# Two value products in a row instead of one at a time, a ring of ten exponential buffers, and a compact layout of the stationary values

## The chip, the cores and the metric

The kernel runs on one core of one Trainium2 chip. The metric is the device time of one execution in microseconds; of several executions the median is given.

## The reference

A layer with attention and a mixture of experts runs on X of 32 batches x 256 tokens x 128 features (float32), both branches from the same normalised input:

```python
xn = _layernorm(x)
x = x + attention(xn) + experts(xn)

# attention, H = 16 heads of DK = 8
ctx = X @ We.T                                          # 16 features
influence = einsum('bqe,bke->bqk', ctx, ctx)
scores = einsum('bhqd,bhkd->bhqk', Q, K) * DK**-0.5 + 0.1 * influence[:, None]
out = softmax(scores) @ V  ->  (b, s, d) @ Wo.T

# experts: 8 of 128 -> 512 -> 128 with gelu, the best 2 of softmax(xn @ gate_w.T) for each token
```

## The kernel before

The engines' programs are written out by hand; each engine runs its own list in order, and semaphores (`wait_ge`, `then_inc`) tie the lists together. After a start (normalising, routing) the attention of batches 0 to 15 runs, then the experts (about 300 to 493 us of the profile), then the attention of batches 16 to 31, while the rows of the experts are gathered.

The attention loop runs over steps `k`, one batch a step, and in each over eight sub-steps `u` = 0 to 7. Work of several batches overlaps in a step: `b` is the batch whose scores are made, `b1_` the next one, `bo` the one before, `b3_` the third ahead. What an engine does in a step, in its order:

- TensorE (PE). At even `u`, two **plain products** for batch `b1_` (`plain(u)`, `plain(u+1)`, L1137, four matmuls each), from which only the maxima of the scores are taken. They go into the two buffers `MX[0]` and `MX[1]`; `plain(v)` waits until VectorE has reduced the product two before it (L1133). At each `u`, two **score products** for batch `b` (`shifted(0)` and `shifted(1)`, L1125, two matmuls each, score products 2u and 2u+1 of the batch) into two banks; score product n waits for the exponential n-2 (L1122). Between the two score products stand small products: those of the values at `u` = 3 (L1147, which wait for `lo_qk` of L966, since they share the bank `MISC`), the transposes of the sums `O` at `u` = 5 (L1154), those of the normalised output at `u` = 7 (L1159). After the score products: at `u` = 0 the output projection of the batch before that (L1185), at `u` = 1 the projection of queries and keys for `b3_` (L1023).
- The **value products** (`values`, L1103) multiply the exponentials by the values: four groups a batch, each of four exponentials, 8 matmuls in float32 with 32 stationary columns, which the profile shows as 16 records in four quads. Group 0 stands at the end of `u` = 2, group 1 at `u` = 4, group 2 at `u` = 6, and group 3 at `u` = 0 of the next step, behind the output projection. Groups 0 and 1 add up in the bank `PV`, are copied to `O` and are followed by groups 2 and 3 there.
- VectorE (DVE). One reduce per plain product (L948, called here the first to eighth reduce of a step), four small transposes of the maxima after the fourth and the eighth (L954), at `u` = 0 the addition of the finished output (L962) after the first reduce, at `u` = 2 `lo_qk` (L966) after the third, at `u` = 5 the reciprocal and the normalising (L972, L976) after the sixth. The reciprocal waits for the transposes of L1154.
- ScalarE (ACT). Sixteen exponentials a step (L700) into a ring `A` of eight buffers, with a wait for a value product (L696); copies of `PV` (L689) at `u` = 1 and 5, `hi_qk` (L706) at `u` = 1, the values into `V` (L716) at `u` = 3, `oT` (L731) at `u` = 7. In the first half it also converts pieces of the experts' weights.
- SyncE issues the loads and stores, GpSimd scatters rows (first half) and gathers them (second half); both are paced by counts of finished score products (`s_ex`).

In the last step, `k` = 31, there are no plain products, and the scores use six banks.

Of the kernel before, what the change touches and what calls it, by code (L numbers as in the profile page):

```python
# [19 lines left out]
F32 = mybir.dt.float32  # L20
F16 = mybir.dt.float16
# [3 lines left out]
ACT = mybir.ActivationFunctionType  # L25
AX = mybir.AxisListType

P = 128
D = 128
B = 32  # L30
S = 256
H = 16
DK = D // H
DE = D // 8
# [6 lines left out]
ET = 2 * B * S // SLOT + NE - 1  # L41
EW = -(-ET // 4)
EP = 4 * EW
NA = 8
VB = 272
DIGIT = 3
QROW, CROW, REST = (0, 9 * DK), (3 * DK, 12 * DK), 5 * DK
MROWS = ((0, 8 * DK), (8 * DK, 14 * DK))
# [2 lines left out]
WS = 2.0 ** 8  # L51
FS = 2.0 ** 10
SCALE = DK ** -0.5
CTX = (0.1 / SCALE) ** 0.5
RW = 2 * D + 2
ZROWS = 9
# [68 lines left out]
def build(nc, X, Wsmall, Wo, W12, B1, B2, out):  # L125
    with ExitStack() as ctx:
        def sb(name, shape, dt):
            return ctx.enter_context(nc.sbuf_tensor(name, shape, dt))
# [12 lines left out]
        x = sb("x", [P, NT, D], F32)  # L141
# [7 lines left out]
        b1 = sb("b1", [P, NE * FC], F32)  # L149
        stack = sb("stack", [P, 2, H, 2, S], F16)  # L150
        A = sb("A", [P, NA, 2, S], F32)
        V = sb("V", [P, 2, 4 * VB], F32)
        O = sb("O", [P, 2, 2, S], F32)
        hi_qk = sb("hi_qk", [P, 2, S], F16)
        lo_qk = sb("lo_qk", [P, 2, S], F16)
# [26 lines left out]


        stats = A[:, 0, :, :].rearrange("p h s -> p (h s)")[:, 0:NT * 6].rearrange("p (t s) -> p t s", s=6)
        zeros = A[:, 1:NA // 2, :, :].rearrange("p n h s -> p (n h s)")[:, 0:ZROWS * RW // 2]
        part_c = [A[:, NA // 2 + r, :, :].rearrange("p h s -> p (h s)").bitcast(F16).rearrange("p (a t) -> p a t", a=2) for r in range(4)]
        early = w12[:, :, :].rearrange("p a n -> p (a n)")
        taken = [0]

# [38 lines left out]
        EX, PV, MISC = bank[4:6], bank[6], bank[7]  # L228
        ring = EX + bank[0:4]

        def scores(k, n):

            return ring[n % len(ring)] if k == B - 1 else EX[n % 2]

        def head_values(par, c, g, i):

            at_ = VB * (2 * c + g % 2) - 16 * (g % 2) + 32 * (4 * (g // 2) + i)
            return V[:, par, at_:at_ + 32]


        s_x = [sem(f"s_x{q}") for q in range(4)]
# [10 lines left out]
        s_qk, s_hq, s_lq, s_cx, s_ch, s_cl, s_v, s_vc = (sem(n) for n in ("s_qk", "s_hq", "s_lq", "s_cx", "s_ch", "s_cl", "s_v", "s_vc"))  # L252
# [4 lines left out]
        s_ex, s_xp, s_pv, s_pe = (sem(n) for n in ("s_ex", "s_xp", "s_pv", "s_pe"))  # L257
# [188 lines left out]
        def _(pool):  # L446
# [36 lines left out]
            pool.memset(V[:, :, :], 0.0).then_inc(s_post, 1)  # L483
            pool.wait_ge(s_post, 4)
            for par in range(2):
                ins = pool.memset(V[:, par, :].rearrange("p (n j) -> p n j", n=4)[:, :, 0:256].rearrange("p n (j d) -> p n j d", d=32)[:, :, :, DK:DK + 1], 1.0)
            ins.then_inc(s_post, 1)

            chain = [0]
# [121 lines left out]
        def _(act):  # L611
# [59 lines left out]
            def attend(s, f, k, first_half=True):  # L671
                b, par, half = s.at(0)
                b1_, par1, _ = s.at(1)
                b3_, par3, _ = s.at(3)
                bo, paro, _ = s.at(-1)
                ch, c_lo = high_chunk(s, k, first_half), low_chunk(s, k, first_half)
                for u in range(8):
                    g = u // 2
                    if first_half and k == HALF and u in (0, 2):
                        experts.load((u // 2 + 1) * (EW // 2))  # L680
                    if first_half and k == HALF and u == 3:
                        act.wait_ge(s_small, 32)
                        act.activation(probe[:, :], ones16[0:1, 0:1], ACT.Gelu_apprx_tanh)
                    if (u == 1 and f["o"]) or (u == (6 if k == B - 1 else 5) and f["x"]):
                        bb, pp, gg = (bo, paro, 1) if u == 1 else (b, par, 0)
                        act.wait_ge(s_pv, 4 * bb + 2 * gg + 2)
                        if k is None or bb >= 2:
                            act.wait_ge(s_ot, bb - 1)
                        act.activation(O[:, pp, gg, :], PV[:, 0:S], ACT.Copy).then_inc(s_pe, 1)  # L689
                    if f["x"]:  # L690
                        for n in (2 * u, 2 * u + 1):
                            act.wait_ge(s_ex, 16 * b + n + 1)
                            if k == 0 and n == 0:
                                act.wait_ge(s_zero, 64)
                            if k != 0 or g >= 2:
                                act.wait_ge(s_pv, 4 * b + g - 1)  # L696
                            if k == 0 and n == NA // 2:
                                for sm in s_cw:
                                    act.wait_ge(sm, 96)
                            act.activation(A[:, n % NA, :, :].rearrange("p h s -> p (h s)"), scores(k, n)[:, :], ACT.Exp, scale=SCALE).then_inc(s_xp, 1)  # L700

                    if u == 1 and f["p"]:
                        act.wait_ge(s_qk, b3_ + 1)
                        if k is None or b3_ >= 1:
                            act.wait_ge(s_wr[1 - par3], 64 * (s.at(2)[2] + 1))
                        act.activation(hi_qk[:, :, :].rearrange("p a t -> p (a t)"), MISC[:, :], ACT.Copy, scale=1 / WS).then_inc(s_hq, 1)  # L706
                    if k == -1 and u == 5:
                        act.wait_ge(s_sub, 3)
                        act.activation(Ex, Dl, ACT.Exp, scale=1 / WS).then_inc(s_exp8, 1)
                        act.wait_ge(s_sub, 4)  # L710
                        act.activation(second, second, ACT.Exp, scale=1 / WS).then_inc(s_exp8, 1)
                    if u == 3 and f["m"]:
                        act.wait_ge(s_v, b1_ + 1)
                        if k is None or b1_ >= 2:
                            act.wait_ge(s_pv, 4 * b1_ - 4)
                        act.activation(V[:, par1, :].rearrange("p (n j) -> p n j", n=4)[:, :, 0:256].rearrange("p n (j d) -> p n j d", d=32)[:, :, :, 0:DK],  # L716
                                       MISC[:, 0:S].rearrange("p (n j d) -> p n j d", n=4, d=DK), ACT.Copy, scale=1 / WS).then_inc(s_vc, 1)
                    if u == 2 and c_lo is not None:
                        act.activation(w_stage[:, :], w_stage[:, :], ACT.Copy, scale=FS).then_inc(s_wsc, 1)
                    if k == 1 and u == 6:  # L720
                        act.wait_ge(s_routed, 2)
                        act.wait_ge(s_place, 2)
                    if u == 6 and ch is not None:
                        act.wait_ge(s_wst, 16 * (ch + 1))
                        dst = w12[:, 0, ch * WCH:(ch + 1) * WCH] if isinstance(ch, int) else w12[:, 0, bass.ds(ch * WCH, WCH)]
                        act.activation(dst, w_stage[:, :], ACT.Copy, scale=FS).then_inc(s_whi, 1)
                    if u == 7 and f["o"]:
                        act.wait_ge(s_oT, bo + 1)
                        if k is None or bo >= 1:
                            act.wait_ge(s_wo, bo)  # L730
                        act.activation(oT[:, :], MISC[:, 0:2 * P], ACT.Copy).then_inc(s_oTe, 1)  # L731
# [279 lines left out]
        def _(pe):  # L1011
# [75 lines left out]
            def attend(s, f, k):  # L1087
# [5 lines left out]
                def values(bb, pp, g):  # L1093

                    gg, e = g // 2, g % 2
                    pe.wait_ge(s_xp, 16 * bb + 4 * g + 4)
                    if g == 0:
                        pe.wait_ge(s_vc, bb + 1)
                    if e == 0 and (not isinstance(bb, int) or 2 * bb + gg >= 1):
                        pe.wait_ge(s_pe, 2 * bb + gg)  # L1100
                    for c in range(2):
                        for i in range(4):
                            mm = pe.matmul(PV[32 * i:32 * i + 32, 0:S], head_values(pp, c, g, i), A[:, (4 * g + 2 * c + i // 2) % NA, i % 2, :],  # L1103
                                           start=(e == 0 and c == 0), stop=(e == 1 and c == 1))
                    mm.then_inc(s_pv, 1)

# [3 lines left out]
                for u in range(8):  # L1110
# [67 lines left out]
                        pe.wait_ge(s_routed, 1)  # L1178
                        experts.load(EW)
                    if u == 0 and f["o"] and closing:  # L1180
                        values(bo, paro, 3)
                    if u == 0 and f["c"]:
                        drained(0, s, f, k)
                        for q in range(2):
                            mm = pe.matmul(MISC[:, S + q * P:S + (q + 1) * P], oT[:, q * P:(q + 1) * P], wo[:, :], start=True, stop=True)  # L1185
                        mm.then_inc(s_wo, 1)
                    if u == 0 and f["o"] and not closing:
                        values(bo, paro, 3)
                    if u == 1 and opening:
                        pe.wait_ge(s_fy, ET)  # L1190
                    if u == 1 and f["p"]:
# [3 lines left out]
                        if k == 1:  # L1195
                            pe.wait_ge(s_routed, 2)
                        project(b3_)
                    if u in ((3, 5, 7) if k == B - 1 else (2, 4, 6)) and f["x"]:
                        values(b, par, g - 1)
                    if k == 0 and u == 6:  # L1200
                        pe.wait_ge(s_vc, 2)
                        pe.wait_ge(s_te, 1)
                        pe.matmul(MISC[0:1, 0:EW], tile_of[0:EP, 0:1], digits[:, :], start=True, stop=True).then_inc(s_tile, 1)
# [78 lines left out]
```

## Time and profile before

| | us |
|---|---|
| runs shown, median of 3 | 711.17 (710.17 to 714.66) |
| the profiled execution, its own time | 710.7 |
| its span, first to last instruction | 708.9 |
| PE busy | 645.0 (91%) |
| DVE busy | 613.8 (87%) |
| ACT busy | 540.8 (76%) |
| GpSimd busy | 469.0 (66%) |
| granted TensorE clock, mean share of full speed | 0.982 |

The busy time of PE is modelled: matmuls are pipelined, and each record holds the time until its last result. Two matmuls that start 0.11 us apart each last 0.27 us, so a busy PE can still have unused places.

### The profile page before, as it was taken

The page shows a single profiled execution, that of the slowest core. Times are in us where ns is not written, and L with a number is a line of the kernel's source. Part 1 is how long each engine was busy: PE and PEld are TensorE (multiplying, and loading weights), DVE is VectorE, ACT ScalarE, POOL GpSimd, SP SyncE. Part 2 cuts the span into 40 slices and gives each one's busy share as a digit, 9 for nine tenths or more (in the row PEclk, how much of TensorE's full clock was granted, in tenths as well). Part 3 has the DMA queues.
Part 4 walks back from the last instruction along what each step waited for, and adds up shares of the span by engine and source line. Part 5 has one row for each costly group of instructions (what it writes and reads, how often), then busy time and mean ns, then how long its engine had stood idle before and what let it go on. Part 6 is the DMA issues. An engine that isn't in the chain of part 4 may idle for free.

```text
span 708.9 us, 22900 instructions
## 1 busy us (share of the span) xinstructions
PE 645.0 (91%) x7800; PEld 431.6 (61%) x7800; DVE 613.8 (87%) x1106; ACT 540.8 (76%) x1123; POOL 469.0 (66%) x542
## 2 busy tenths in 40 slices
PE   0367899999999999879999999999999999999996
PEld 0254445555555555569999999999455555555553
DVE  8979899999899899758888888887999999999991
ACT  2583478888888888758888888888787887778785
POOL 8680478687677657125566566566688888878883
PEclk9996799999999999999999999999999999999999
DMA  9859566676686776564444454543576877788742
GB/s 249 305 161 338 150 160 180 179 204 167 178 199 178 184 183 172 148 109 100 101 106 102 101 96 110 103 99 79 142 169 174 191 186 187 175 189 195 179 112 76
DMA packets 162975, 113.71 MB, mean 160 GB/s; under 512 B 72624, under 2 KB 150448, under 8 KB 162864
## 3 DMA queue, kind: packets, MB, share of 16 engines
q1 hardware_dynamic: 153632, 90.63, 51.5%
q0 software_dynamic: 8192, 16.86, 9.8%
q10 hardware_dynamic: 1040, 4.76, 1.8%
q8 instruction: 67, 1.10, 0.7%
q14 instruction: 44, 0.36, 0.2%
HBM read 55.42 MB, written 47.19 MB: 145 GB/s over the span
## 4 chain that ended last, share of the span: by engine, by line
PE 62%; DVE 16%; SPq 9%; DMA 7%; issue 4%; ACT 1%; DVEq 0%; ACTq 0%
PE bank L1243 14%; PE mx L1232 13%; PE bank L1125 12%; PE bank L1103 10%; DVE mx L948 8%; PE mx L1137 6%; DMA stack<-qk_dram 4%; PE bank L1023 2%; PE bank L1185 2%; DVE A L783 2%; SPq L322 2%; DVE lo_qk L966 2%; DMA stack<-mT 2%; SPq L326 1%; PE bank L1154 1%
## 5 line engine op out<-in xcount | busy, mean ns | idle before, releaser
L700 ACT ACTIVATE A<-bank 128x512 f32<-128x512 f32 x502 | 278.0, 597 | 57.6 <-PE bank L1125 48.7
L948 DVE TENSOR_REDUCE mx<-mx 128x4 f16<-128x1024 f32 x256 | 302.5, 1205 | 18.4 <-PE mx L1137 15.9
L571 POOL TENSOR_SCALAR rows<-rows,slot_p 128x128 f32<-128x128 f32 x142 | 112.2, 800 | 99.0 <-DVE rows L999 99.0
L1125 PE MATMUL bank<-stack 113*128 113x256 f16 x1004 | 170.1, 276 | 1.8 <-ACT A L700 0.8
L557 POOL DMA_INDIRECT slots_x<-rows,pos x128 | 124.0, 969 | 50.9 <-PE bank L1125 30.0
L601 POOL DMA_INDIRECT rows<-slots_y,pos x128 | 122.0, 953 | 37.1 <-issue 18.2
L1103 PE MATMUL bank<-A,V 128*32 128x256 f32 x2048 | 137.1, 385 | 1.8 <-ACT A L700 1.7
L744 ACT ACTIVATE rows<-mx,b 128x256 f32<-128x256 f32 x284 | 111.5, 475 | 30.2 <-PE mx L1232 29.9
L1125 PEld LDWEIGHTS bank<-stack 113*128 113x128 f16 x1004 | 73.2, 97 | 89.6 <-ACT A L700 48.7
L993 DVE TENSOR_TENSOR rows<-rows 128x512 f16<-128x512 f32 x142 | 101.2, 714 | 24.5 <-ACT rows L748 22.1
L1243 PE MATMUL bank<-w,rows 128*128 x1704 | 108.4, 220 | 4.4 <-DVE rows L993 4.4
L1243 PEld LDWEIGHTS bank<-w,rows 128*128 128x128 f16 x1704 | 102.2, 98 | 6.7 <-issue 4.9
L1232 PE MATMUL mx<-rows,w 128*128 128x256 f16 x852 | 105.1, 273 | 0.0
L1137 PE MATMUL mx<-stack 64*128 64x256 f16 (+1 forms) x1024 | 88.4, 277 | 11.8 <-DVE mx L948 5.9
L1232 PEld LDWEIGHTS mx<-rows,w 128*128 x852 | 80.6, 98 | 8.5 <-issue 0.2
L1103 PEld LDWEIGHTS bank<-A,V 128*32 128x32 f32 x2048 | 53.5, 109 | 48.5 <-issue 20.0
L1137 PEld LDWEIGHTS mx<-stack 64*128 64x128 f16 (+1 forms) x1024 | 33.4, 95 | 59.1 <-DVE mx L948 26.2
L954 DVE STREAM_TRANSPOSE mT<-mx 32x32 f16<-32x32 f16 x256 | 51.2, 200 | 4.8
L748 ACT ACTIVATE rows<-rows 128x512 f16<-128x512 f32 x71 | 44.8, 631 | 6.7
L1044 PE MATMUL mx<-ident,rows 128*128 128x128 f16 x128 | 13.9, 274 | 35.5 <-DVE rows L820 33.9
L689 ACT ACTIVATE O<-bank 128x256 f32<-128x256 f32 x64 | 24.7, 386 | 27.8 <-PE bank L1103 27.8
L989 DVE CAST rows<-rows 128x512 f16<-128x512 f32 x71 | 30.4, 428 | 12.7 <-ACT rows L744 5.7
(142 smaller groups left out, 591.4 us busy)
## 6 DMA issues: line engine op xcount, KB each, us to landing
stack<-ctx_rest SPq DMA_DIRECT2D x64, 256.0 KB
stack<-qk_dram SPq DMA_DIRECT2D x128, 96.0 KB
slots_y<-rows SPq DMA_DIRECT2D x71, 128.0 KB, 2.1
qk_dram<-hi_qk SPq DMA_DIRECT2D x64, 128.0 KB
stack<-ctx_high SPq DMA_DIRECT2D x128, 64.0 KB
slots_x<-A ACTq DMA_DIRECT2D x1, 4644.0 KB, 19.8
w_stage<-in_w SPq DMA_DIRECT2D x8, 512.0 KB
qk_dram<-lo_qk SPq DMA_DIRECT2D x64, 64.0 KB
```

The lines of the kernel that those rows point to most:

```text
L557: pool.indirect_dma_start(slots_x, bass.IndirectOffsetOnAxis(pos[j][:, t:t + 1], 0), rows[:, t, :].bitcast(F32), None).then_inc(s_scat, 16)
L571: ins = pool.tensor_scalar(ye[n % 4][:, h, :], ye[n % 4][:, h, :], slot_p[:, n // 4 % 3, n % 4, h:h + 1], None, ALU.mult)
L601: pool.indirect_dma_start(ye2[n % 2][:, m, :], None, slots_y, bass.IndirectOffsetOnAxis(pos[j][:, t:t + 1], 0)).then_inc(s_yg[n % 2][m], 16)
L700: act.activation(A[:, n % NA, :, :].rearrange("p h s -> p (h s)"), scores(k, n)[:, :], ACT.Exp, scale=SCALE).then_inc(s_xp, 1)
L744: act.activation(h32[r % 2][:, fc, :], bank[fc][:, 0:SLOT], ACT.Gelu_apprx_tanh, bias=b1[:, bass.ds(e + fc, 1)], scale=1 / FS).then_inc(s_ ...
L948: dve.tensor_reduce(mx[:, a, 8 * qt:8 * qt + 8].rearrange("q (i e w) -> q i e w", i=2, e=2)[:, :, g % 2], MX[u % 2][:, :].rearrange("q (i ...
L993: dve.tensor_tensor(lo, h, hi, ALU.subtract).then_inc(s_fl, 1)
L1103: mm = pe.matmul(PV[32 * i:32 * i + 32, 0:S], head_values(pp, c, g, i), A[:, (4 * g + 2 * c + i // 2) % NA, i % 2, :], start=(e == 0 and c ...
L1125: mm = pe.matmul(scores(k, n)[:, i * S:(i + 1) * S], stack[0:SHIFT + 1, par, h, 1, c * P:(c + 1) * P], stack[0:SHIFT + 1, par, h, 0, :], s ...
L1137: mm = pe.matmul(MX[v % 2][:, (2 * i + p) * S:(2 * i + p + 1) * S], stack[r0:r1, par1, h, 0, v % 2 * P:(v % 2 + 1) * P], stack[r0:r1, par1 ...
L1232: mm = pe.matmul(bank[fc][:, 0:SLOT], w1[:, pa, bass.ds(e + fc * P, P)], xt[r][:, pb, :], start=(n == 0), stop=(n == 2))
L1243: mm = pe.matmul(bank[6 + par][:, h * D:(h + 1) * D], hp[par][:, pa, fc, h * P:(h + 1) * P], w2[:, pb, bass.ds(e_before + fc * P, P)], sta ...
```

## The change

On PE, groups 0 and 1 of the value products now stand one behind the other at the end of `u` = 4, groups 2 and 3 one behind the other at `u` = 0 of the next step, again behind the output projection; at `u` = 2 and `u` = 6 there are none. The last step keeps its order, and so do all waits of `values` itself. The ring `A` has ten buffers and goes on from batch to batch, so that an exponential waits for the value product of ten exponentials before. `V` shrinks from 1088 to 768 columns: each 48-column place holds the values of two heads, 16 zeros apart. ACT copies the values at `u` = 4, behind the exponentials 8 and 9, instead of `u` = 3. The order of the rows of Wv is changed on the host.

```diff
-NA = 8
-VB = 272
+NA = 10
+VP = 3 * 2 * DE // 2
...
-        V = sb("V", [P, 2, 4 * VB], F32)
+        V = sb("V", [P, 2, H * VP], F32)
...
-            at_ = VB * (2 * c + g % 2) - 16 * (g % 2) + 32 * (4 * (g // 2) + i)
+            at_ = VP * (8 * c + 4 * (g // 2) + i) + 16 * (g % 2)
             return V[:, par, at_:at_ + 32]
...
-                            if k != 0 or g >= 2:
-                                act.wait_ge(s_pv, 4 * b + g - 1)
-                            if k == 0 and n == NA // 2:
+                            if 16 * b + n >= NA:
+                                act.wait_ge(s_pv, (16 * b + n - NA) // 4 + 1)
+                            if k == 0 and n == 4:
...
-                            act.activation(A[:, n % NA, :, :].rearrange("p h s -> p (h s)"), scores(k, n)[:, :], ACT.Exp, scale=SCALE).then_inc(s_xp, 1)
+                            act.activation(A[:, (16 * b + n) % NA, :, :].rearrange("p h s -> p (h s)"), scores(k, n)[:, :], ACT.Exp, scale=SCALE).then_inc(s_xp, 1)
...
-                    if u == 3 and f["m"]:
+                    if u == 4 and f["m"]:
                         act.wait_ge(s_v, b1_ + 1)
...
-                        act.activation(V[:, par1, :].rearrange("p (n j) -> p n j", n=4)[:, :, 0:256].rearrange("p n (j d) -> p n j d", d=32)[:, :, :, 0:DK],
-                                       MISC[:, 0:S].rearrange("p (n j d) -> p n j d", n=4, d=DK), ACT.Copy, scale=1 / WS).then_inc(s_vc, 1)
+                        act.activation(head_columns(par1), MISC[:, 0:S].rearrange("p (n e d) -> p n e d", e=2, d=DK), ACT.Copy, scale=1 / WS).then_inc(s_vc, 1)
...
                     if u == 0 and f["o"] and closing:
-                        values(bo, paro, 3)
+                        for n in ((3,) if bo == B - 1 else (2, 3)):
+                            values(bo, paro, n)
...
                     if u == 0 and f["o"] and not closing:
-                        values(bo, paro, 3)
+                        for n in (2, 3):
+                            values(bo, paro, n)
...
-                    if u in ((3, 5, 7) if k == B - 1 else (2, 4, 6)) and f["x"]:
+                    if f["x"] and k == B - 1 and u in (3, 5, 7):
                         values(b, par, g - 1)
+                    if f["x"] and k != B - 1 and u == 4:
+                        for n in range(2):
+                            values(b, par, n)
```

## Rows read from the trace of the kernel before

**Rows 1.** The page: busy time of the engines, and granted clock in 40 slices.
```profile
PE 645.0 (91%) x7800; PEld 431.6 (61%) x7800; DVE 613.8 (87%) x1106; ACT 540.8 (76%) x1123; POOL 469.0 (66%) x542
...
PEclk9996799999999999999999999999999999999999
```

**Rows 2.** Busy us by stretch: length, PE, PEld, DVE, ACT, POOL, clock, DMA share, GB/s.
```profile
202.13:215.25 13.12, 13.00 (x150) 6.91 (x148) 12.41 (x22) 11.04 (x22) 9.91 (x12) 1.00 0.84 208
560.00:640.00 80.00, 78.98 (x910) 43.53 (x908) 75.33 (x124) 63.73 (x129) 65.84 (x65) 1.00 0.78 184
```

**Rows 3.** Line L948: what its idle time before waited for, who waited (us, times).
```profile
  PE mx L1137: 15.9, 25
...
  PEld mx L1137: 26.2, 72
```

**Rows 4.** Timeline of DVE, one step: start, us, instruction, count, idle before.
```profile
205.39 1.23 DVE L948 TENSOR_REDUCE mx<-mx 128x4 f16<-128x1024 f32 x1 [0.50 <-PE mx L1137]
206.53 0.68 DVE L966 SCALAR_TENSOR_TENSOR lo_qk<-bank,hi_qk 128x512 f16<-128x512 f32 x1
207.13 1.22 DVE L948 TENSOR_REDUCE mx<-mx 128x4 f16<-128x1024 f32 x1
...
209.15 2.30 DVE L948 TENSOR_REDUCE mx<-mx 128x4 f16<-128x1024 f32 x2
211.38 0.34 DVE L972 RECIPROCAL rden<-bank 128x32 f32<-128x32 f32 x1
...
212.09 2.35 DVE L948 TENSOR_REDUCE mx<-mx 128x4 f16<-128x1024 f32 x2
...
218.88 1.23 DVE L948 TENSOR_REDUCE mx<-mx 128x4 f16<-128x1024 f32 x1 [0.87 <-PE mx L1137]
```

**Rows 5.** Timeline of DVE, end of the next step and its successor's third reduce.
```profile
225.58 2.35 DVE L948 TENSOR_REDUCE mx<-mx 128x4 f16<-128x1024 f32 x2
...
231.99 1.23 DVE L948 TENSOR_REDUCE mx<-mx 128x4 f16<-128x1024 f32 x1 [0.49 <-issue]
```

**Rows 6.** Timeline of PE over the same boundary: value product, scores, projection, plain products.
```profile
229.35 1.07 PE L1103 MATMUL bank<-A,V 128*32 128x256 f32 x16
230.36 0.61 PE L1125 MATMUL bank<-stack 113*128 113x256 f16 x4
230.81 0.82 PE L1023 MATMUL bank<-xT,ws 128*128 128x256 f16 x6
231.56 0.61 PE L1137 MATMUL mx<-stack 64*128 64x256 f16 x8
```

**Rows 7.** Timeline of PE, the fourth and fifth sub-steps (u = 4, 5).
```profile
208.40 0.39 PE L1137 MATMUL mx<-stack 64*128 64x256 f16 x4
208.72 0.61 PE L1125 MATMUL bank<-stack 113*128 113x256 f16 x4
209.26 1.07 PE L1103 MATMUL bank<-A,V 128*32 128x256 f32 x16
210.27 0.39 PE L1125 MATMUL bank<-stack 113*128 113x256 f16 x2
210.50 0.60 PE L1154 MATMUL bank<-ident,O 128*128 128x128 f32 x4
```

**Rows 8.** Timeline of the weight loads (PEld): the second plain product at u = 4.
```profile
208.39 0.12 PEld L1137 LDWEIGHTS mx<-stack 64*128 64x128 f16 x4 [0.36 <-DVE mx L948]
```

**Rows 9.** Timeline of PE in two very short windows: third and fourth quad.
```profile
206.49 0.40 PE L1103 MATMUL bank<-A,V 128*32 128x256 f32 x4
...
206.71 0.40 PE L1103 MATMUL bank<-A,V 128*32 128x256 f32 x4
```

**Rows 10.** Timeline of PE, u = 3: the products of the values.
```profile
207.27 0.51 PE L1147 MATMUL bank<-ws,xT 128*128 128x128 f16 x6
```

**Rows 11.** The page's groups: exponentials, busy, mean ns, and what their idle time waited for.
```profile
L700 ACT ACTIVATE A<-bank 128x512 f32<-128x512 f32 x502 | 278.0, 597 | 57.6 <-PE bank L1125 48.7
```

**Rows 12.** Timeline of ACT: the copy of the values.
```profile
208.53 0.38 ACT L716 ACTIVATE V<-bank 128x256 f32<-128x256 f32 x1
```

More of the change, by code:

```diff
@@ L184, in build @@
         stats = A[:, 0, :, :].rearrange("p h s -> p (h s)")[:, 0:NT * 6].rearrange("p (t s) -> p t s", s=6)
-        zeros = A[:, 1:NA // 2, :, :].rearrange("p n h s -> p (n h s)")[:, 0:ZROWS * RW // 2]
-        part_c = [A[:, NA // 2 + r, :, :].rearrange("p h s -> p (h s)").bitcast(F16).rearrange("p (a t) -> p a t", a=2) for r in range(4)]
+        zeros = A[:, 1:4, :, :].rearrange("p n h s -> p (n h s)")[:, 0:ZROWS * RW // 2]
+        part_c = [A[:, 4 + r, :, :].rearrange("p h s -> p (h s)").bitcast(F16).rearrange("p (a t) -> p a t", a=2) for r in range(4)]
         early = w12[:, :, :].rearrange("p a n -> p (a n)")
@@ L235, in head_values, with head_columns @@
         def head_values(par, c, g, i):
-            at_ = VB * (2 * c + g % 2) - 16 * (g % 2) + 32 * (4 * (g // 2) + i)
+            at_ = VP * (8 * c + 4 * (g // 2) + i) + 16 * (g % 2)
             return V[:, par, at_:at_ + 32]
+        def head_columns(par):
+            v = V[:, par, 0:DK]
+            return bass.AP(v.tensor, v.offset, [list(v.ap[0]), [VP, H], [32, 2], [1, DK]])
         s_x = [sem(f"s_x{q}") for q in range(4)]
@@ L485, in _ @@
             for par in range(2):
-                ins = pool.memset(V[:, par, :].rearrange("p (n j) -> p n j", n=4)[:, :, 0:256].rearrange("p n (j d) -> p n j d", d=32)[:, :, :, DK:DK + 1], 1.0)
+                ins = pool.memset(V[:, par, :].rearrange("p (n j) -> p n j", j=VP)[:, :, DK:VP:32], 1.0)
             ins.then_inc(s_post, 1)
@@ L1102, in values @@
                         for i in range(4):
-                            mm = pe.matmul(PV[32 * i:32 * i + 32, 0:S], head_values(pp, c, g, i), A[:, (4 * g + 2 * c + i // 2) % NA, i % 2, :],
+                            mm = pe.matmul(PV[32 * i:32 * i + 32, 0:S], head_values(pp, c, g, i), A[:, (16 * bb + 4 * g + 2 * c + i // 2) % NA, i % 2, :],
                                            start=(e == 0 and c == 0), stop=(e == 1 and c == 1))
@@ L1260 @@
     from concourse.bass_utils import run_bass_kernel_spmd
-    wv = np.asarray(L0_attn_Wv).reshape(2, 2, 4, DK, D).transpose(1, 0, 2, 3, 4).reshape(D, D)
+    wv = np.asarray(L0_attn_Wv).reshape(2, 2, 4, DK, D).transpose(0, 2, 1, 3, 4).reshape(D, D)
     wq, wk = (np.asarray(w).reshape(2, 2, 2, 2, DK, D).transpose(4, 0, 2, 1, 3, 5).reshape(D, D) for w in (L0_attn_Wq, L0_attn_Wk))
```

## The prediction

> **What bounds the kernel now.** The page's busy times come first: PE is busy for 91% of the span, DVE for 87%, ACT for 76% [rows 1]. Read alone, they name PE. The view by stretch seems to say the same, PE 13.00 us in a step of 13.12 in the first half and 78.98 in 80 us of the second; but DVE stands at 12.41 of 13.12 and 75.33 of 80, close behind [rows 2]. A PE time holds the drain of each matmul, so it can be full of places where PE waits. The question is which engine waits last, and the view of the reduce's line answers it: in the whole kernel the reduces wait for plain products 25 times, 15.9 us in total, while weight loads of plain products wait for a reduce 72 times, 26.2 us [rows 3].
>
> The timeline of DVE shows where. In a step, DVE idles at one place, ahead of the third reduce: 0.50 us, 0.87 and 0.49 in three steps in a row [rows 4, 5]. From the third reduce (205.39) to the end of the eighth (212.09 + 2.35 = 214.44) everything stands end to end, 9.05 us [rows 4]. Then PE leads: the second plain product of the next step needs the buffer that the eighth reduce frees, and behind it, in PE's order, come two score products, the output projection, value product 3, two score products, the projection, and only then the plain product that the third reduce waits for. From the end of the eighth reduce (225.58 + 2.35 = 227.93) to the next third reduce (231.99) it is 4.06 us [rows 5], of which value product, scores and projection take 231.56 - 229.35 = 2.21 [rows 6]. So a step is a loop, 9.05 us of DVE and 4.06 of PE: 13.11 us, and 0.38 more where ACT converts weights (0.87 against 0.49). What is added to PE between the eighth and the third reduce lengthens the step in full. What is taken from PE elsewhere gives nothing unless DVE waits there.
>
> **The change part by part.** *One value product behind another.* Quads of a value product start 206.71 - 206.49 = 0.22 us apart [rows 9], so a product of four that follows another adds 4 x 0.22 = 0.88 us. Alone it costs more: from its start to the next score product 210.27 - 209.26 = 1.01 [rows 7], and at its entry another 0.09 (four score matmuls and then a value product take 209.26 - 208.72 = 0.54, four before the projection 230.81 - 230.36 = 0.45 [rows 6, 7]). So 1.10 alone, 0.88 behind another: PE saves 0.22 us a pair, 0.44 a step. I take 0.88, as the next quad needs the same kind of weights and the same tiles; the bound from the other side is 1.10.
>
> The Trainium skill, "TensorEngine Tiling (Array Packing)", Key Properties, says that a change of the tiling mode drains the engine. The entry and exit rows agree, and by that rule alone the change is a gain; it is the first rival below.
>
> *Groups 2 and 3 at u = 0 (+0.88 a step).* Group 2 now stands inside the PE leg of the loop. Nothing leaves that leg: the scores, the projections and their waits stay. DVE has no other work there, since its lists for `u` = 0 and 1 are done before it idles. The step grows by 0.88 wherever a step has both a `bo` and plain products: k = 1 to 15 and 17 to 30, 29 steps, 25.5 us.
>
> *Nothing at u = 2 (0).* After the scores of `u` = 2, PE now comes 1.1 us early to `u` = 3. There the products of the values wait for `lo_qk`, which ends at 206.53 + 0.68 = 207.21; they start at 207.27, 0.06 later [rows 4, 10]. The value product of `u` = 2 thus hid in that wait, and its place is idle afterwards. `lo_qk` follows the third reduce, so it can't come sooner.
>
> *Groups 0 and 1 at u = 4 (+0.66 a step).* The second plain product of `u` = 4 waits for the fourth reduce (weights at 208.39 after 0.36 us of waiting [rows 8], reduce done at 207.13 + 1.22 = 208.35 [rows 4]), so PE can't start `u` = 4 sooner. Then come two score products, the value products, a score product and the transposes of `O`, ending at 210.50 + 0.60 = 211.10 [rows 7]; the reciprocal runs at 211.38, when DVE is free [rows 4]. With 0.88 more the transposes end at 211.98, and with the 0.06 from result to waiting engine that `lo_qk` showed, the reciprocal starts at 212.04: 0.66 late. What is queued behind it on DVE is the seventh and eighth reduce, and behind these the second plain product of the next step. So this 0.66 goes into the loop too: 29 x 0.66 = 19.1 us. The next plain products don't add to it: on PE they follow the transposes behind one score product, while DVE is at the reciprocal and the normalising, 212.09 - 211.38 = 0.71 us [rows 4].
>
> *Nothing at u = 6 (0).* PE comes early to the next step's plain products, which wait for the seventh and eighth reduce, now later still.
>
> *The ring of ten (0).* Idle time of ACT before the exponentials goes to score products, 48.7 of 57.6 us, and none is shown against a value product [rows 11]. The ring is needed for the later release: exponential 10 wants group 0 done, which PE finishes ahead of score product 10. Neither wait costs.
>
> *The copy of the values at u = 4 (0).* It takes 0.38 us and stood ahead of exponential 8 [rows 12]; now it lies behind exponential 9, while PE does 1.9 us of value products and needs no new exponential. The transposes of `u` = 5 wait for it, but come later by 0.88. Uncovered, it would cost 0.38 a step. The shape written has as many elements; a slower form up to twice as long still fits.
>
> *Smaller memset, permuted Wv, other places in V (0).* The memset is GpSimd's, before the attention; Wv is permuted on the host; the stationary operand stays 128 x 32.
>
> *Ends (+1).* In the steps where ACT converts weights, exponentials come about 0.2 us later still through the shorter cover at `u` = 6 (7 steps, some +1); k = 0, 16 and 31 have one of the effects each, of either sign, under 1 us each. Bounds -2 to +4.
>
> Sum: 25.5 + 19.1 + 1 = 45.6 us. On the profiled execution's 710.7 us this gives 756.3; that execution lies 0.5 under the median of the runs shown. I predict 756 us, with 748 to 764 as this case's own range.
>
> **The rivals.**
> - *PE is the bound, and the switches saved count.* Then 0.44 us a step for 31 steps goes, 13.6 us: 697. For it speak PE's 13.00 of 13.12 us [rows 2]. Against it: DVE's idle time is one wait a step for PE, at just the place where the change adds work [rows 4, 5], and even without any such wait only 15.9 us could go [rows 3]. It decides if PE's leg after the eighth reduce isn't lengthened, so if the third reduce starts no later after it than 4.06 us. 4%.
> - *The transposes are not late.* If something lets PE into `u` = 4 about 0.7 us earlier, the second term goes and 25.5 + 1 stays: 737. Against it stands the wait of rows 8. 10%.
> - *A second value product costs as much as the first.* If the groups don't run together (the waits in `values` lie between them), 0.22 is added to both terms, 29 x 0.44 = 12.8: 769. For it: nothing shows two in a row in this trace. Against it: the quads within one follow at an even pace. 8%.
> - *The exponentials become a further link.* At `u` = 6 and 7 scores now wait for exponentials of 0.6 us with no value product as cover. PE saves the 1.10 us of that product; exponentials of 0.597 us [rows 11], two in flight, take about half back by my estimate, so PE still stands some 0.6 us ahead of the end of the eighth reduce. If the chain is longer by 0.9, 0.3 is added a step, 9 us: 765. 8%.
> - *No change.* All of it falls into waits. That needs slack ahead of the third reduce, and there DVE is already idle: 711. 2%.
>
> **How the numbers follow.** My case has 68%, the rivals 4, 10, 8, 8 and 2. The prediction is that of the likeliest, 756. The range goes from 735 to 771: it takes in the case without the transposes' delay below and both additions above, and leaves out about 6% below and some above. About 1% (7 us) is what a measurement of this kernel can tell from no change. Faster by over 1%: 4%; within 1%: 2%; slower: 94%.
>
> **What would show it.** The wait ahead of the third reduce grows from 0.5 to about 1.4 us a step; a new wait of DVE for L1154 of some 0.6 us stands ahead of the reciprocal; a step takes about 14.65 us instead of 13.11 (15.2 instead of 13.49 with a weight conversion). PE's busy share falls, though the value products themselves cost less, 16 records becoming 32 that span about 1.95 us. The experts' stretch is as long as before. Wrong would be: third reduces that don't wait longer; reciprocals right behind the sixth reduce; value products of a pair with a gap between them; or a granted clock below the 1.00 of rows 2 in the attention, as PE now idles more.

## The result, and the profile after

The changed kernel takes 751.03 us in the median (749.73 to 751.33) against 711.61 of the kernel before on the same chip: 1.0545 times as long, 95% interval 1.0507 to 1.0582. The forecast was 756, range 735 to 771, slower.

The page of the changed kernel, its busy times, the reduces and the reciprocals (busy, mean ns | idle before, released by):

```profile
span 749.1 us, 22898 instructions
...
PE 649.9 (87%) x7800; PEld 438.6 (59%) x7800; DVE 615.8 (82%) x1106; ACT 542.1 (72%) x1123; POOL 466.4 (62%) x542
...
PEclk9965999999999999999999999999999999999998
...
L952 DVE TENSOR_REDUCE mx<-mx 128x4 f16<-128x1024 f32 x256 | 302.6, 1204 | 41.6 <-PE mx L1141 40.9
```

The busy times of all engines are within 5 us of those of [rows 1], those of the weight loads, which overlap PE, within 7; yet the span grew by 749.1 - 708.9 = 40.2 us. So no engine has much more to do; engines wait longer. The reduces wait for plain products 40.9 us instead of 15.9 [rows 3]. With all causes taken together, the groups by line have 18.4 us of idle time before the reduces in the kernel before and 41.6 now, 23.2 more. The other part is ahead of the reciprocal. First the kernel before, the group of the reduces and what the reciprocal's line waited for, then the reciprocal's line now:

```profile
L948 DVE TENSOR_REDUCE mx<-mx 128x4 f16<-128x1024 f32 x256 | 302.5, 1205 | 18.4 <-PE mx L1137 15.9
...
  PE bank L1154: 6.1, 5
```

```profile
L976 DVE RECIPROCAL rden<-bank x32: 357/358/358, 103.3 to 742.8; 128x32 f32<-128x32 f32 x32
...
  PE bank L1158: 19.0, 25
  issue: 3.9, 7
```

That is 22.9 us against 6.1, 16.8 more. The two together, 23.2 + 16.8 = 40.0, are the 40.2 us of the span. (Line numbers are four to five higher than before: L952 is the reduce, L1141 the plain products, L1107 the value products, L1129 the scores, L1158 the transposes of `O`, L976 the reciprocal.)

A step of the changed kernel in the timeline of DVE, to be read beside [rows 4]:

```profile
208.04 0.36 DVE L976 RECIPROCAL rden<-bank 128x32 f32<-128x32 f32 x1 [0.59 <-issue]
...
215.99 1.22 DVE L952 TENSOR_REDUCE mx<-mx 128x4 f16<-128x1024 f32 x1 [1.30 <-PE mx L1141]
217.13 0.68 DVE L970 SCALAR_TENSOR_TENSOR lo_qk<-bank,hi_qk 128x512 f16<-128x512 f32 x1
217.73 1.21 DVE L952 TENSOR_REDUCE mx<-mx 128x4 f16<-128x1024 f32 x1
...
219.75 2.30 DVE L952 TENSOR_REDUCE mx<-mx 128x4 f16<-128x1024 f32 x2
222.60 0.36 DVE L976 RECIPROCAL rden<-bank 128x32 f32<-128x32 f32 x1 [0.55 <-issue]
222.99 0.42 DVE L980 TENSOR_TENSOR o_n<-bank,rden 128x256 f32<-128x256 f32 x1
223.33 2.35 DVE L952 TENSOR_REDUCE mx<-mx 128x4 f16<-128x1024 f32 x2
...
231.16 1.23 DVE L952 TENSOR_REDUCE mx<-mx 128x4 f16<-128x1024 f32 x1 [1.83 <-PE mx L1141]
...
237.81 0.36 DVE L976 RECIPROCAL rden<-bank 128x32 f32<-128x32 f32 x1 [0.59 <-PE bank L1158]
```

There are two waits where there was one: 1.30 us ahead of the third reduce (0.49 in [rows 5]; 1.83 in the steps after a weight conversion, 0.87 in [rows 4]) and a new one of 0.55 ahead of the reciprocal. From one reciprocal to the next a step takes 222.60 - 208.04 = 14.56 us, and 237.81 - 222.60 = 15.21 with a weight conversion, against 13.11 and 13.49 before; the forecast named 14.65 and 15.2. The same step on PE:

```profile
211.50 0.61 PE L1129 MATMUL bank<-stack 113*128 113x256 f16 x4
211.95 0.61 PE L1190 MATMUL bank<-wo,oT 128*128 128x128 f32 x4
212.49 1.93 PE L1107 MATMUL bank<-A,V 128*32 128x256 f32 x32
214.35 0.61 PE L1129 MATMUL bank<-stack 113*128 113x256 f16 x4
...
215.55 0.61 PE L1141 MATMUL mx<-stack 64*128 64x256 f16 x8
216.10 0.61 PE L1129 MATMUL bank<-stack 113*128 113x256 f16 x4
217.18 0.39 PE L1129 MATMUL bank<-stack 113*128 113x256 f16 x2 [0.47 <-ACT A L705]
217.87 0.51 PE L1151 MATMUL bank<-ws,xT 128*128 128x128 f16 x6 [0.29 <-DVE lo_qk L970]
...
219.86 1.93 PE L1107 MATMUL bank<-A,V 128*32 128x256 f32 x32
221.73 0.39 PE L1129 MATMUL bank<-stack 113*128 113x256 f16 x2
221.96 0.60 PE L1158 MATMUL bank<-ident,O 128*128 128x128 f32 x4
```

Two value products in a row take 214.35 - 212.49 = 1.86 us to the next score product, and with one entry of 0.09 it is 1.95. Two single ones take 2 x 1.01 and two entries of 0.09 [rows 6, 7], 2.20. So a pair saves 0.25 us of PE. The saving is real. But the place at `u` = 2 that the value product left is now idle, 0.47 us for an exponential and 0.29 for `lo_qk`, and the time was added where DVE waits.

### The profile page after: what moved, and what is told of

The parts are those of the page before. It is cut to its first block, busy times and chain, and to the rows that moved or that the text cites. A ratio compares the mean times of both kernels' runs of the same rounds, so it can differ in the third digit from the quotient of the medians.

```text
span 749.1 us, 22898 instructions
## 1 busy us (share of the span) xinstructions
PE 649.9 (87%) x7800; PEld 438.6 (59%) x7800; DVE 615.8 (82%) x1106; ACT 542.1 (72%) x1123; POOL 466.4 (62%) x542
## 4 chain that ended last, share of the span: by engine, by line
PE 59%; DVE 23%; issue 9%; ACT 3%; SPq 2%; POOL 2%; DMA 2%; ACTq 0%; DVEq 0%; POOLq 0%
PE bank L1107 14%; PE bank L1252 13%; PE mx L1241 12%; DVE mx L952 11%; PE bank L1129 9%; PE mx L1141 5%; DVE lo_qk L970 3%; ACT A L705 2%; PE bank L1027 2%; PE bank L1190 2%; POOL w L516 2%; DVE A L787 2%; PE bank L1158 2%; DMA stack<-qk_dram 1%; DVE o_n L980 1%
## 5 line engine op out<-in xcount | busy, mean ns | idle before, releaser
L952 DVE TENSOR_REDUCE mx<-mx 128x4 f16<-128x1024 f32 x256 | 302.6, 1204 | 41.6 <-PE mx L1141 40.9
L1129 PE MATMUL bank<-stack 113*128 113x256 f16 x1004 | 170.9, 275 | 31.3 <-ACT A L705 30.6
L1129 PEld LDWEIGHTS bank<-stack 113*128 113x128 f16 x1004 | 70.3, 97 | 114.5 <-ACT A L705 57.3
L1107 PE MATMUL bank<-A,V 128*32 128x256 f32 x2048 | 124.2, 382 | 2.2 <-ACT A L705 2.1
L1141 PE MATMUL mx<-stack 64*128 64x256 f16 (+1 forms) x1024 | 89.8, 276 | 11.5 <-DVE mx L952 8.2
L1107 PEld LDWEIGHTS bank<-A,V 128*32 128x32 f32 x2048 | 60.0, 109 | 46.4 <-issue 7.2
L1141 PEld LDWEIGHTS mx<-stack 64*128 64x128 f16 (+1 forms) x1024 | 34.8, 95 | 59.0 <-DVE mx L952 28.9
```

The source lines that it names most:

```text
L952: dve.tensor_reduce(mx[:, a, 8 * qt:8 * qt + 8].rearrange("q (i e w) -> q i e w", i=2, e=2)[:, :, g % 2], MX[u % 2][:, :].rearrange("q (i ...
L1129: mm = pe.matmul(scores(k, n)[:, i * S:(i + 1) * S], stack[0:SHIFT + 1, par, h, 1, c * P:(c + 1) * P], stack[0:SHIFT + 1, par, h, 0, :], s ...
L1141: mm = pe.matmul(MX[v % 2][:, (2 * i + p) * S:(2 * i + p + 1) * S], stack[r0:r1, par1, h, 0, v % 2 * P:(v % 2 + 1) * P], stack[r0:r1, par1 ...
```

## The experiments

My theory: a step is a loop of DVE (third to eighth reduce) and a leg of PE (from the end of the eighth reduce to the plain products that the third one reads). A value product added to the leg is paid in full, one added at `u` = 4 as far as the transposes come late, and PE work elsewhere is free. The main rival: PE's total work and its switches set the time.

**Layout, ring and copy alone (e1).** The value products go back to their old places:

```diff
-                        for n in (2, 3):
-                            values(bo, paro, n)
+                        values(bo, paro, 3)
...
-                    if f["x"] and k != B - 1 and u == 4:
-                        for n in range(2):
-                            values(b, par, n)
+                    if f["x"] and k != B - 1 and u in (2, 4, 6):
+                        values(b, par, g - 1)
```

> The changed kernel with the value products back at their old places (u = 2, 4, 6 and 0 of the next step): ring of ten, compact V and the copy of the values at u = 4 remain. My theory: these parts cost nothing, 711 us, the wait ahead of the third reduce stays at 0.5 us a step and the reciprocal waits for nothing. Rival, that the layout (ring, copy, stationary values at new distances) carries part of the loss: 715 to 750.

Measured: 714.78 us, 1.0024 (1.0004 to 1.0045) times the kernel before. Nearly nothing, but not quite: the third reduce waits 0.58 us instead of 0.49. The first row is DVE, the second, from another step, the weight loads of PE:

```profile
551.63 1.23 DVE L952 TENSOR_REDUCE mx<-mx 128x4 f16<-128x1024 f32 x1 [0.58 <-PE mx L1141]
```
```profile
570.01 0.42 PEld L1158 LDWEIGHTS bank<-ident,O 128*128 128x128 f32 x4 [0.19 <-ACT V L721]
```

The transposes of `u` = 5 wait for the copy of the values. That can be undone by itself (e8):

```diff
-                    if u == 4 and f["m"]:
+                    if u == 3 and f["m"]:
                         act.wait_ge(s_v, b1_ + 1)
```

> As e1, with the copy of the values on ACT back at u = 3. In e1 a step takes 13.20 us instead of 13.11. If that comes from the copy behind exponential 9 (it holds back the transposes of u = 5 and, through the exponentials, oT and the output projection in the PE leg), the step is 13.11 us again and the time 710 to 713, as before. If the ring or the compact layout slows the exponentials or the value products, the step stays at 13.20 and the time 2 to 3 us above the kernel before.

Measured: 710.83 us, 0.9978 (0.9955 to 1.0001), the wait again 0.49:

```profile
540.73 1.22 DVE L952 TENSOR_REDUCE mx<-mx 128x4 f16<-128x1024 f32 x1 [0.49 <-issue]
```

So ring and compact layout cost nothing that shows; the moved copy costs about 0.09 us a step where nothing else is late. The last link is on record: the weights of the output projection, in the leg, wait for `oT` 30 times in e1 (6.9 us) and 12 times in e8 (3.7 us). How e1's late transposes make `oT` late was not followed there; e3 below shows such a chain.

**The pair at u = 0 alone (e2), the pair at u = 4 alone (e3).**

```diff
 e2:
-                    if f["x"] and k != B - 1 and u == 4:
-                        for n in range(2):
-                            values(b, par, n)
+                    if f["x"] and k != B - 1 and u in (2, 4):
+                        values(b, par, g - 1)
 e3:
-                        for n in (2, 3):
-                            values(bo, paro, n)
+                        values(bo, paro, 3)
...
                     if f["x"] and k != B - 1 and u == 4:
                         for n in range(2):
                             values(b, par, n)
+                    if f["x"] and k != B - 1 and u in (6,):
+                        values(b, par, g - 1)
```

> Groups 2 and 3 together at u = 0 as in the changed kernel, groups 0 and 1 at u = 2 and u = 4 as before. My theory: only the PE leg between the eighth and the third reduce is longer, by 0.8 to 0.95 us in 29 steps, so 735 us; the third reduce waits 1.3 us a step, the reciprocal for nothing. Rival, that PE's total work counts (0.22 us a step saved at the switches): 704 us.

> Groups 0 and 1 together at u = 4 as in the changed kernel, group 2 at u = 6 and group 3 at u = 0 as before. My theory: only the reciprocal is late, by about 0.55 us in 29 steps, so 727 us; the wait ahead of the third reduce stays near 0.5. Rival (PE's total work counts): 704 us. The two halves together, e2 and e3, should make up the 40 us of the change.

Measured: e2 733.90 us, 1.0283 (1.0262 to 1.0304); e3 732.74 us, 1.0270 (1.0253 to 1.0287). The increases, 2.83% and 2.70%, make 5.53% together; the whole change made 5.45%. In the steps they fit less well: e2 adds 0.81 us to a step (13.92), e3 0.82 (13.93), 1.63 together, and the whole change 1.45. That the percentages agree so closely is in part luck. Third reduce and reciprocal in the timelines of DVE, first e2, then e3:

```profile
551.06 1.23 DVE L952 TENSOR_REDUCE mx<-mx 128x4 f16<-128x1024 f32 x1 [1.30 <-issue]
...
557.06 0.34 DVE L976 RECIPROCAL rden<-bank 128x32 f32<-128x32 f32 x1
```
```profile
550.59 1.23 DVE L952 TENSOR_REDUCE mx<-mx 128x4 f16<-128x1024 f32 x1 [0.68 <-PE mx L1141]
...
557.20 0.36 DVE L976 RECIPROCAL rden<-bank 128x32 f32<-128x32 f32 x1 [0.55 <-PE bank L1158]
```

Each half has the wait that it was to have. Both save PE time at one pair and both are slower, which ends the first rival. e3 is nearly 6 us above its expectation: its third reduce waits 0.68 us and not 0.5. In the leg the output projection waits for ACT:

```profile
603.05 0.52 PEld L1189 LDWEIGHTS bank<-wo,oT 128*128 128x128 f32 x4 [0.16 <-ACT oT L735]
```

The lost time lies at this place: from the score products ahead of the output projection to the value product behind it PE takes 1.18 us (546.77 to 547.95), in the kernel before 0.99 (546.89 to 547.88). The projection waits for `oT` 31 times in e3 (7.2 us), but 12 times (3.8 us) in the kernel before and 12 times (3.8 us) in the changed kernel; so this part of e3 isn't in the whole change. The way there can be followed by the times. From the late transposes on PE has no pause up to the last score product but one of the batch. Against the end of the eighth reduce (546.42 before, 546.35 in e3) this score product (545.36, 545.47), the exponential behind it (545.79, 545.89) and `oT` behind the exponentials (546.76, 546.86) all come 0.17 to 0.18 us later in e3. That link I had left out. In the changed kernel no value product stands at `u` = 6, and PE has made up the delay by then: a plain product waits for a reduce again (0.19 us at 211.18).

**Group 3 behind the leg (e4).** e3, with group 3 at `u` = 2 of the next step:

```diff
-                    if (u == 1 and f["o"]) or (u == (6 if k == B - 1 else 5) and f["x"]):
-                        bb, pp, gg = (bo, paro, 1) if u == 1 else (b, par, 0)
+                    late = 3 if f["x"] else 1
+                    if (u == late and f["o"]) or (u == (6 if k == B - 1 else 5) and f["x"]):
+                        bb, pp, gg = (bo, paro, 1) if u == late else (b, par, 0)
...
-                    if u == 0 and f["o"] and not closing:
+                    if u == 2 and f["o"] and not closing:
                         values(bo, paro, 3)
```

> As e3, but group 3 moves from u = 0 to u = 2 of the next step (behind the plain products that the third reduce needs), its copy from PV to u = 3. The work of PE is that of e3. My theory of the loop: the PE leg loses 1.1 us, of which 0.5 can be used since DVE then has no wait there; the reciprocal's 0.55 stays: 13.15 us a step, 709 to 714 us in all. Rival, that PE's total work or the number of its switches sets the time: the same as e3.

Measured: 721.82 us, 1.0107 (1.0088 to 1.0126). With the same work on PE it is 11 us faster than e3, so the place counts and not the total. It is 8 us above the upper end of my expectation. The weight loads of PE in the leg show why:

```profile
596.11 0.11 PEld L1130 LDWEIGHTS bank<-stack 113*128 113x128 f16 x2 [0.37 <-ACT A L706]
596.60 0.55 PEld L1028 LDWEIGHTS bank<-xT,ws 128*128 128x128 f16 x6 [0.38 <-DVE x L967]
```

Without a value product as cover, a score product waits for its exponential and the projection for DVE's addition of the output. Of the 1.1 us that the leg lost, a step got back 13.93 - 13.38 = 0.55, and a wait of some 0.1 us is left ahead of the third reduce: two reduces that take about 1.22 each stand in one row of 2.56 us, where two in a row without a wait take 2.30 to 2.35.

```profile
542.96 2.56 DVE L953 TENSOR_REDUCE mx<-mx 128x4 f16<-128x1024 f32 x2
...
550.90 0.36 DVE L977 RECIPROCAL rden<-bank 128x32 f32<-128x32 f32 x1 [0.54 <-PE bank L1159]
...
564.28 0.36 DVE L977 RECIPROCAL rden<-bank 128x32 f32<-128x32 f32 x1 [0.54 <-PE bank L1159]
```

The reciprocal's wait is that of e3 and costs 0.64 us a step, as in the changed kernel. So the step takes 564.28 - 550.90 = 13.38 us and not the 13.15 that I expected: against the 13.11 of before, 0.64 is added at the reciprocal and some 0.38 gained at the third reduce.

**The same extra work inside and outside the leg (e5, e6).** Eight matmuls whose result is not used, in the kernel before at the end of `u` = 1, in the changed kernel at the end of `u` = 2:

```diff
+                    if u == 1 and f["o"] and f["x"] and k != B - 1:      # e6: u == 2
+                        pe.wait_ge(s_pe, 2 * bo + 2)
+                        for n in range(8):
+                            pe.matmul(PV[:, S:2 * S], ws[:, 0, 0:P], xT[:, 0, 0:S], start=True, stop=True)
```

> The kernel before with eight more matmuls of 128 x 128 by 256 columns (0.87 us; their result is not used) on PE at the end of u = 1, in 29 steps, behind the projection and ahead of the plain products of u = 2: inside the PE leg. My theory: the whole 0.87 us a step is paid, 711 + 25 = 736 us, as a wait ahead of the third reduce of 1.4 us. Rival, that PE's total work sets the time: 736 us as well.

> The changed kernel with the same eight matmuls on PE at the end of u = 2, where the change took a value product away, in 29 steps. My theory: PE idles there (for an exponential and for lo_qk), so the 0.87 us a step are free, 751 us, at most 2 us more. Rival, that PE's total work sets the time: 751 + 25 = 776 us.

Measured: e5 736.54 us, 1.0345 (1.0298 to 1.0392), 24 us more than before, 0.83 a step. e6 751.64 us, 1.0561 (1.0511 to 1.0611), no more than the changed kernel without them (1.0545, 1.0507 to 1.0582). Third reduce of e5:

```profile
212.62 1.23 DVE L948 TENSOR_REDUCE mx<-mx 128x4 f16<-128x1024 f32 x1 [1.37 <-PE mx L1137]
```

PE in e6, to be read beside the PE rows of the changed kernel above:

```profile
216.33 0.61 PE L1129 MATMUL bank<-stack 113*128 113x256 f16 x4
216.78 1.04 PE L1212 MATMUL bank<-xT,ws 128*128 128x256 f16 x8
217.65 0.38 PE L1129 MATMUL bank<-stack 113*128 113x256 f16 x2
218.10 0.51 PE L1151 MATMUL bank<-ws,xT 128*128 128x128 f16 x6
```

The eight matmuls stand where the two waits were, and the products of the values start 218.10 - 215.79 = 2.31 us after the plain products of `u` = 2 (215.79 in e6), as without them (217.87 - 215.55 = 2.32). 29 x 0.87 = 25 us of PE work are free at one place and cost 24 us at the other. e5 alone would fit the rival too; e6 doesn't. The two stand on different kernels: the same work at `u` = 2 of the kernel before, or at `u` = 1 of the changed one, was not run.

**Shortening the leg instead (e7).** If the leg costs, then taking something out of it should pay. In the kernel before the projection of queries and keys goes behind the plain products of `u` = 2:

```diff
 PE:
-                    if u == 1 and f["p"]:
-                        drained(1, s, f, k)
...
-                        project(b3_)
...
                         for v in (u, u + 1):
                             plain(v)
+                    if u == 2 and f["p"]:
+                        drained(1, s, f, k)
...
+                        project(b3_)
...
-                        if u == 3 and f["m"]:
+                        if u == 4 and f["m"]:
                             drained(3, s, f, k)
 DVE, ahead of the four transposes of u = 3:
-                    if u == 2 and f["p"]:
+                    if u == 3 and f["p"]:
                         b3_ = s.at(3)[0]
```

> The kernel before with the projection of queries and keys moved out of the PE leg, behind the plain products of u = 2; lo_qk on DVE behind the fourth reduce, the products and the copy of the values at u = 4 instead of u = 3. The value products stand where they stood. My theory of the loop: the leg is 0.75 us shorter, the third reduce waits for nothing, and the step falls to DVE's own 12.6 to 12.8 us: 695 to 705 us. Rival, that PE's total work sets the time: no change, 711. A second rival: the projection's followers (hi_qk, lo_qk, the products of the values) come late in their new places and open a wait that eats the gain: 708 to 725.

Measured: 717.24 us, 1.0068 (1.0042 to 1.0095): a small loss where my theory had 695 to 705, and within what the second rival gave. A step by DVE, the busy times of that step (columns as in [rows 2]), and a weight load of PE in it:

```profile
579.76 3.59 DVE L948 TENSOR_REDUCE mx<-mx 128x4 f16<-128x1024 f32 x3
...
587.47 0.36 DVE L973 RECIPROCAL rden<-bank 128x32 f32<-128x32 f32 x1 [0.50 <-PE bank L1155]
```
```profile
578.22:591.36 13.14, 13.06 (x152) 7.13 (x150) 12.44 (x21) 10.43 (x22) 10.96 (x11) 1.00 0.76 187
```
```profile
581.03 0.12 PEld L1138 LDWEIGHTS mx<-stack 64*128 64x128 f16 x4 [0.36 <-DVE mx L948]
```

The wait ahead of the third reduce is gone (three reduces in one row), as the loop says. But a wait of 0.50 us stands ahead of the reciprocal instead: the projection now lies on PE's way to the transposes, and the step is 13.14 us, or 13.91 with a weight conversion against 13.49. What the leg gave back, this second stretch took. PE's own list isn't shown to be the bound, in spite of its 13.06 us of 13.14: in the same step a plain product waits for DVE's second reduce (the row at 581.03), and behind it come the moved projection and the rest up to the transposes. I read it as a second loop through DVE and PE; how long PE's list would be without such waits no run shows. No run here clearly beats the kernel before.

## Why the prediction was right

*What bounds.* The step as said: the one wait of DVE ahead of the third reduce grew, and nothing else on DVE but the reciprocal. The 0.25 us that a pair saves on PE gave no time, since it fell into waits. What the loop doesn't tell is the gain from a shorter leg: e4 got back 0.55 of 1.1 us a step, e7 nothing, because other waits came up. The Trainium skill, "TensorEngine Tiling (Array Packing)", Key Properties, says that a change of the tiling mode drains the engine. The saved 0.25 us a pair agrees with it; no run separates a drain from other costs of the change.

*Groups 2 and 3 at u = 0.* Forecast 0.88 a step; measured 1.30 - 0.49 = 0.81, and 1.83 - 0.87 = 0.96 after a weight conversion. e2 alone gave the same 1.30. Over 29 steps 0.81 is 23.5 us, against 25.5. The second product added 1.86 - 1.01 = 0.85, and PE was 0.06 sooner at the first one: from the end of the eighth reduce to the value product PE took 229.35 - 227.93 = 1.42 us before [rows 5, 6] and 212.49 - (208.78 + 2.35) = 1.36 after.

*Groups 0 and 1 at u = 4.* Forecast 0.66; the reciprocal waits 0.55 us, and from the third reduce to the end of the eighth DVE takes 223.33 + 2.35 - 215.99 = 9.69 us against 9.05, so 0.64. Over 29 steps 18.6 us against 19.1.

*u = 2, u = 6, ring, layout.* Nothing, as forecast; e6 and e8 show it. *The copy of the values.* Forecast 0; 0.09 a step in the old order (e1). In the changed kernel the transposes of `O` wait for it nowhere: the view of their line names DVE alone, 4 times, as in the kernel before.

```profile
  DVE x L966: 2.6, 4
```

The changed kernel with the copy back at `u` = 3 was not run.

*Ends.* Forecast +1, within -2 to +4; measured 40.2 - 23.5 - 18.6 = -1.9, as a sum of both signs, so that it lies within the bounds by luck. The seven steps with a weight conversion add 15.21 - 13.49 = 1.72 each, 0.27 more than the others, 1.9 in all. From the reciprocal of step 15 to that of step 16 it is 1.0 more. At the start the changed kernel gains 2.8. First the kernel before, then the changed one:

```profile
93.62 0.25 DVE L918 TENSOR_SCALAR tile_e<-bank 1x18 int32<-1x18 f32 x2 [0.96 <-PE bank L1203]
```
```profile
90.78 0.24 DVE L922 TENSOR_SCALAR tile_e<-bank 1x18 int32<-1x18 f32 x2
```

Of these 93.62 - 90.78 = 2.84 us, 1.19 was there at the first reduce (66.59 against 65.40), before any product that moved; over all runs here it starts between 65.18 and 66.59. The wait of 0.96 us, for a product behind the value product of `u` = 6, is gone with that value product: it is gone in e2 and e6 too and there in e3. Most of the rest is a wait of 0.62 us, which e5 lacks as well though it keeps the order of before.

The sum was also wrong about two of its 29 steps. In steps 29 and 30 no batch is left to project, so the leg is shorter, and in the kernel before the third reduce didn't wait there. The third reduce of step 29, before (the second of three in one row) and after (the first of two):

```profile
667.29 3.48 DVE L948 TENSOR_REDUCE mx<-mx 128x4 f16<-128x1024 f32 x3
```
```profile
706.64 2.36 DVE L952 TENSOR_REDUCE mx<-mx 128x4 f16<-128x1024 f32 x2 [0.64 <-PE mx L1141]
```

There the steps grew by 0.92 and 0.89 us and not by 1.45, 1.1 less in all. So what is added to the leg is paid in full only where DVE already waits for it, and the prediction's "lengthens the step in full" was too wide by this condition.

So the sum was 45.6 us and the spans differ by 40.2: 2.0 too much for the first term, 0.5 for the second, 2.9 for the ends. The clock, which could have upset it, was granted at 1.00 in the attention as before; a step of the changed kernel (columns as in [rows 2]):

```profile
215.99:231.16 15.17, 13.42 (x154) 7.25 (x150) 12.50 (x21) 11.42 (x24) 8.64 (x10) 1.00 0.62 179
```

*The rivals.* PE as the bound (697) fell by e2, e3 and e6. Transposes that are not late (737) fell by the new wait for L1158. A second product at the price of the first (769) fell by the 1.86 us. Exponentials as a further link (765) don't show in the changed kernel's sum; in e4 a score product waits for one in the leg, and in e3 they pass the delay on to `oT`.

## What to carry to other kernels

A busy share of 91% did not say that PE was the bound. Find the stretch in which the last engine waits, and ask which instructions lie between the release and the wait: here work added there was paid nearly in full wherever the waiting engine was already idle, while work of the same length a few instructions on was free in the changed kernel. Putting like work together saves switches on one engine, but it also makes two long stretches out of four short ones, and what waited behind a short one now waits behind a long one.

## What the runs showed of the hardware

A reduce in a row on DVE starts 0.07 to 0.08 us before the one ahead has ended (in [rows 4], 2.30 us for two of about 1.2). After a wait this overlap is lost and the reciprocal takes 0.36 us instead of 0.34, so that an idle time of 0.55 us before it cost 0.64.
